# Hyena block with a gated FFN: down-weight loads at their own step of POOL's queue, first stage's tables redrawn

## The reference

```python
xn = layernorm(x)                                   # eps 1e-5
# attention branch: a second layernorm, with gamma and beta
proj = (layernorm(xn, gamma, beta) @ W_in + b_in)   # 256 -> 3 * 256: v, x1, x2
y = conv(v, k0) * x1                                # causal, 128 taps, per channel
y = conv(y, k1) * x2
attn = xn + (y @ W_out + b_out)
# FFN branch: integer weights times 1/127, hidden size 768
ffn = (silu(xn @ w_gate.T) * (xn @ w_up.T)) @ w_down.T
out = x + attn + ffn
```

## Time and profile before

| | us |
|---|---|
| median of 3 runs (325.54 to 327.3) | 325.62 |
| the profiled execution | 325.64 |
| its span | 323.7 |
| TensorE busy | 300.2 |
| VectorE busy | 264.6 |
| POOL busy | 210.0 |
| ScalarE busy | 184.4 |

### The profile page before, as it was taken

One profiled execution on the slowest core, in us unless ns is written; L12 is line 12 of the kernel. 1 busy time (PEld: TensorE's weight loads), 2 busy tenths in 40 slices (PEclk: granted clock), 3 DMA queues, 4 the chain that ended last, 5 costly groups with the idle time before them and its releaser, 6 DMA issues.

```text
span 323.7 us, 11895 instructions
## 1 busy us (share of the span) xinstructions
PE 300.2 (93%) x4945; PEld 235.9 (73%) x4945; DVE 264.6 (82%) x490; ACT 184.4 (57%) x398; POOL 210.0 (65%) x290
## 2 busy tenths in 40 slices
PE   0778999999999999999999999999999999999993
PEld 0366889977677777868777777877777867668982
DVE  2799999759886978886897989879787877879994
ACT  2769999644544445452554454354445344679990
POOL 4698997687877876968787776868778573100000
PEclk9999999999999999999999999999999999999998
DMA  7995005898796787869687687968678789002344
GB/s 229 350 349 113 2 0 149 371 374 339 283 377 230 316 299 270 357 225 382 205 337 276 281 315 253 375 220 367 232 306 309 276 357 330 26 1 68 132 165 163
DMA packets 22033, 81.01 MB, mean 250 GB/s; under 512 B 1494, under 2 KB 13402, under 8 KB 13786
## 3 DMA queue, kind: packets, MB, share of 16 engines
q1 hardware_dynamic: 19458, 77.47, 63.9%
q0 software_dynamic: 2368, 2.36, 3.7%
q10 hardware_dynamic: 152, 0.40, 0.4%
HBM read 75.50 MB, written 4.72 MB: 248 GB/s over the span
## 4 chain that ended last, share of the span: by engine, by line
PE 37%; POOL 18%; DVE 17%; issue 12%; ACT 11%; DMA 3%; POOLq 0%; SPq 0%; DVEq 0%
PE bank_c L324 12%; PE bank_p L324 7%; PE bank_u L324 5%; PE bank_g L324 5%; DVE sgh L1047 5%; PE bank_d L324 5%; POOL ybuf L1381 4%; ACT vx L838 4%; DVE hhl L1052 4%; ACT hhl L757 3%; POOL res L1333 3%; ACT vx L830 3%; DMA res<-in_L_attn_x 3%; POOL res L1334 2%; DVE ybuf L1068 2%
## 5 line engine op out<-in xcount | busy, mean ns | idle before, releaser
L324 PE MATMUL bank_d<-wd,hhl 128*128 128x256 f16 x384 | 84.2, 271 | 0.2 <-DVE res L1059 0.2
L324 PEld LDWEIGHTS bank_p<-wq,xT 128*128 128x128 f16 x1536 | 69.3, 98 | 14.1
L324 PE MATMUL bank_p<-wq,xT 128*128 128x64 f16 x1536 | 78.5, 193 | 0.0
L324 PE MATMUL bank_g<-xT,wgu 128*128 128x512 f16 x192 | 66.2, 377 | 0.5 <-ACT sgh L751 0.5
L324 PE MATMUL bank_u<-xT,wgu 128*128 128x512 f16 x192 | 66.2, 378 | 0.1
L324 PEld LDWEIGHTS bank_c<-ybuf,bands 128*128 128x128 f16 x1024 | 51.9, 96 | 17.3 <-issue 0.9
L324 PEld LDWEIGHTS bank_c<-vhl,bands 128*128 128x128 f16 x1024 | 48.9, 96 | 18.8 <-issue 3.4
L324 PE MATMUL bank_c<-ybuf,bands 128*128 128x64 f16 (+3 forms) x1024 | 60.5, 184 | 0.6 <-issue 0.6
L757 ACT CAST hhl<-sgh 128x512 f16<-128x512 f32 x48 | 29.7, 618 | 52.4 <-DVE sgh L1047 52.4
L324 PE MATMUL bank_c<-vhl,bands 128*128 128x64 f16 (+3 forms) x1024 | 57.4, 184 | 2.0 <-DVE ybuf L1068 1.0
L1052 DVE TENSOR_TENSOR hhl<-sgh,hhl 128x512 f16<-128x512 f32 x48 | 46.9, 977 | 13.9 <-ACT hhl L757 12.9
(11 more groups left out here) (185 smaller groups left out, 562.1 us busy)
## 6 DMA issues: line engine op xcount, KB each, us to landing
bands<-taps_seq SPq DMA_DIRECT2D x64, 1024.0 KB, 8.2
out<-res SPq DMA_DIRECT2D x8, 512.0 KB, 3.1
res<-in_L_attn_x SPq DMA_DIRECT2D x3, 1024.0 KB, 10.8
res<-in_L_attn_x SPq DMA_DIRECT2D x2, 512.0 KB, 6.1
bands<-in_L_attn_W_in SPq DMA_DIRECT2D x1, 768.0 KB, 6.0
wgu<-in_L_ffn_w_gate POOLq DMA_DIRECT2D x1, 768.0 KB, 8.8
wgu<-in_L_ffn_w_up POOLq DMA_DIRECT2D x1, 768.0 KB, 10.0
wd<-in_L_ffn_w_down POOLq DMA_DIRECT2D x2, 384.0 KB, 10.4
```

Source lines behind the costliest of these rows:

```text
L324: return nc.tensor.matmul(o, w, m, start=start, stop=stop, skip_group_check=True)
```

## The change

The two down loads are taken out of `load_integers` into a function `load_down` with a table entry of its own, INTS_DOWN = 2; INTS becomes 3. In the loop the call of `load_down` stands behind that of `load_integers`. The other tables of the stage get other entries: block 7, 17 and 22 are normalised by POOL, 23 by VectorE, 24 by ScalarE; x1 tile 5 goes to ScalarE and 6 to VectorE; the flip of the second batch moves from block 9 to 8 and second_scales(2) from step 11 to 9.

```diff
@@ -36,27 +36,28 @@
     CR = 32
     NR = D // CR
     CUTS = (0, 4, 8, 16, 24, NB)
-    V_LATE, V_EARLY = 8, 3
-    X_LATE, X_EARLY = 2, 5
+    V_LATE, V_EARLY = 9, 3
+    X_LATE, X_EARLY = 3, 5
     LAST = 44
-    FLIPS = (6, 9, 13, 19, 25)
-    NORM = "AAAAAAAAAPAPPAPPAAVPAAVPPAAPPAPP"
+    FLIPS = (6, 8, 13, 19, 25)
+    NORM = "AAAAAAAPAPAPPAPPAPVPAAPVAAAPPAPP"
     REVERSE = "AAAAAAAAAAVVAAVAVAAAAAAAAVAVAAAV"
-    X1 = "AAAAAVAAVVVVVVAV"
-
-    STATS = {1: 2, 3: 2, 4: 1, 5: 1, 6: 2, 9: 1, 10: 3}
-    WHI, WLO, PLO, SDG, KMAX = 2, 4, 2, 4, 4
-    BETA, BIAS = (2, 5), (5, 12)
-    SCALES_1, SCALES_2 = (5, 10, 18), (4, 8, 11, 15, 24)
-    INTS = 2
+    X1 = "AAAAAAVAVVVVVVAV"
+
+    STATS = {1: 1, 3: 2, 4: 2, 5: 1, 6: 1, 7: 1, 9: 1, 10: 2, 11: 1}
+    WHI, WLO, PLO, SDG, KMAX = 3, 4, 2, 4, 4
+    BETA, BIAS = (2, 4), (5, 12)
+    SCALES_1, SCALES_2 = (5, 10, 18), (4, 8, 9, 15, 24)
+    INTS = 3
+    INTS_DOWN = 2
     TAPS = (11, 16, 17, 23, 24)
     ADD_X2 = (29, 29, 39, 43)
-    ADD_BIAS, ROUND_V, SPLIT_V = (16, 20, 37, 43), (20, 24, 30, 37), (28, 31, 38)
-    MAXIMA = (7, 8, 8, 10, 12, 13, 16, 16, 16)
-    FLAG_PE, FLAG_V = (18, 19), (18, 21, 24, 29)
-    PAIR_PE = (22, 24, 29, 33, 39, 39, 39, 45, 48)
+    ADD_BIAS, ROUND_V, SPLIT_V = (16, 20, 36, 43), (20, 24, 30, 37), (28, 31, 38)
+    MAXIMA = (8, 8, 8, 10, 12, 14, 16, 16, 16)
+    FLAG_PE, FLAG_V = (18, 19), (18, 22, 24, 29)
+    PAIR_PE = (22, 24, 29, 33, 39, 39, 42, 45, 46)
     PAIR_A = (22, 24, 29, 33, 38, 39, 44, 48, 50)
-    PAIR_V = (23, 26, 32, 39, 39, 42, 45, 50, 51)
+    PAIR_V = (23, 26, 32, 37, 40, 42, 45, 50, 51)
     RESIDUALS = (0, 2, 2, 3, 2, 3, 3, 2, 2, 2, 2, 2, 2, 2, 2, 0)
     FORK = 24
     NBATCH = len(CUTS) - 1
@@ -1336,6 +1337,8 @@
             def load_integers():
                 pool.dma_start(gu_f[:, 0:HB, :], w_gate.rearrange("(u p) d -> p u d", p=P)).then_inc(int_loaded[0], 16)
                 pool.dma_start(gu_f[:, HB:2 * HB, :], w_up.rearrange("(u p) d -> p u d", p=P)).then_inc(int_loaded[1], 16)
+
+            def load_down():
                 for a in range(KD):
                     pool.dma_start(wd_f[:, :, a, :], w_down[a * P:(a + 1) * P, :].rearrange("p (j d) -> p j d", d=D)).then_inc(int_loaded[2], 16)
 
@@ -1344,6 +1347,8 @@
             for b in range(2, LAST):
                 if b == INTS:
                     load_integers()
+                if b == INTS_DOWN:
+                    load_down()
                 if b in SCALES_1:
                     first_scales(SCALES_1.index(b) + 2)
                 if b + 2 < NB and NORM[b + 2] == "P":
```

## The result

The changed kernel takes 327.86 us (median of 20 runs, 325.26 to 330.12), the kernel before 326.05 (20 runs, 325.08 to 330.5). The ratio is 1.0053, interval 1.0034 to 1.0072: slower by half a per cent, about 1.7 us. Forecast were 326.7 us and +1.1, with a range of 324.8 to 328.1. The measured 327.86 lies inside it, near the upper edge; the kernel before stood 0.4 us higher in these runs than the 325.62 from which the forecast started. The profiled execution took 326.52 us, its span is 324.7.

A forecast was written before the change was run, and what follows sets the result against it. Bound by TensorE from 33 to 62 us, before that by POOL's chain until 32.65. 325.64 us plus 1.30 + 0.35 - 0.19 - 0.37 = +1.1 gave 326.7 us, range 324.8 to 328.1.

The forecast's parts named there:

- The loads' order: POOL's four DMA issues, down loads first: 3.44 us in either order, gate landing near 25.6, nothing waits; 0 us.
- L945 where it stood, L1254 held up: VectorE's input-weight split again starts at 19.71; POOL's 8-number instruction beside it again lasts about 1.6 us; 0 us.
- rival A: POOL's chain 1.6 us shorter, for instance L1254 not held up (1.42); no wait at block 12; -0.5, 325.1 us; chance 0.18.
- Block 12 ready at 33.2, block 14 at 35.75: POOL normalises block 12 3.0 us later; TensorE waits 1.7 us there and starts block 14 1.30 us later.
- From block 14 to the end: TensorE's remaining work: +0.35 for two late v blocks, -0.19 and -0.37 for waits gone before blocks 18 and 24.
- rival B: ScalarE takes over the first stage's end, some 1.9 us late behind the first pair; stage 1.9 to 2.3 late, 327.7; chance 0.17.
- B's point of decision: TensorE needs block 23's split for block 26; ScalarE decides if it loses 1.5 us more than 1.9.
- The wait ahead of block 24 gone because of the flag: TensorE's 0.37 us wait goes because VectorE now splits block 21 ahead of the flag and scales.
- The sum: All terms together, TensorE's delay through the stage: +1.1 us, giving 326.7 us.
- the forecast's own band: Whole kernel slower by +0.6 to +1.6 us; chance 0.50.
- What moves the first convolution moves the end: TensorE's dense main loop passes on any shift at the first convolution; forecast wrong if the shift at 63 differs from the end's.

The follow-up runs named there:

- the second profile: The changed kernel, unaltered, profiled once more; first convolution at 63.68 us, against 64.06 in its first profile and 62.06 in the kernel before.
- flag run: Changed kernel with VectorE's flag and weight scales back at step 21 instead of 22; ratio 1.0035 (1.0006 to 1.0064).
- the kernel with the three entries back: Changed kernel with block 7 on ScalarE, second_scales(2) at step 11, second batch's flip at block 9 again; ratio 0.9999 (0.9974 to 1.0023).
- the three entries alone: Kernel before with only block 7 on POOL, second_scales(2) at step 9, second batch's flip at block 8; ratio 1.0023 (0.9995 to 1.0051).

## Why the prediction was right or wrong, point by point

- **The loads' order, 0 us.** Right: 3.49 and 3.48 us of issues, gate at 25.8 (forecast 25.6), ratio 1.0005 for it alone.
- **L945 where it stood, L1254 held up.** Right in the changed kernel (19.84; 1.55 us). The fear in rival A was justified: when VectorE starts 0.6 us later and POOL 0.4 earlier, L1254 isn't held up, 0.21 us. But what the prediction said of it, that an earlier L1254 would only hand the block to the power behind, is wrong. The power that began at 19.42 took its 1.64 us, and L946 beside it its 1.81; only the instruction behind the power was held, 0.63 us instead of 0.20. So 1.0 of the 1.42 us is gained.
- **Block 12 ready at 33.2, block 14 at 35.75.** Measured 33.24 (32.68 and 0.56) and 35.80 at full clock, with 1.50 us of standing (forecast 1.7). With the stands ahead of blocks 7 and 8 that the same three entries make, this step carries the result: taking the entries back brings 1.0053 to 0.9999, and block 14 to 34.51.
- **From block 14 to the end, forecast -0.2 us.** Mis-sized. At full clock the shift was +1.35 at block 14, +1.17 at block 24 (47.98 against 46.81), as summed, and then +1.62 at block 28 (53.36; before, 51.74) and at the first convolution. The 0.45 us more come from ScalarE being late. Its rounding of the first pair, block 23, and a reversal, from the second profile:

```profile
47.70 0.71 ACT L714 ACTIVATE wgu<-bank_d,cst 128x512 f16<-128x512 f32 x1
...
48.77 0.39 ACT L688 CAST xT<-bank_d 128x256 f16<-128x256 f32 x1
...
51.96 0.68 ACT L695 COPY xr<-xT 128x512 f16<-128x512 f16 x1
```

  The pair is 1.75 us later than before (45.95) and the rounding of block 23 at 48.77, where rival B said 48.9. B's point of decision (block 26) was not reached, but the reversal that ends at 52.64 releases the x1 product at 52.69, 0.28 us late (it is this wait, and not x1 tile 9, as the flag run's expectation had it). The other 0.16 lies ahead of block 25: the second pair's transposes wait until 49.2 for VectorE's split of the first pair, which could start only behind ScalarE's rounding of it. So a small part of rival B came true beside the forecast. In all, the step from block 14 to the first convolution measures +0.27 us (1.62 less 1.35) where -0.2 was forecast, and +0.55 in the kernel with the three entries back.
- **The wait ahead of block 24 gone because of the flag.** The wait went, the reason was wrong (flag back at step 21).
- **The clock.** Not foreseen. In the first profile it adds 0.4 us at the first convolution. The kernel before has no such fall in the stage (its mean of 0.995 comes from the last 4 us, with 0.59 granted). In the timed runs a lower clock is more frequent after the change: ten of 20 runs have a mean under 0.995, of the kernel before three to five in series of 29 to 35. (A mean doesn't say where in the run the clock fell.) But the loss is there without it: the five runs with a mean of 0.999 took 327.41, 327.68, 328.03, 329.05 and 329.32 us, none of them near the 326.05 of the kernel before.
- **The sum.** +1.6 us at full clock and +2.0 with the dip, against +1.1; the times say 1.7. That is just above the forecast's own band of +0.6 to +1.6 and inside the range given with it. The mechanism was right up to block 14, and what was missed is the half microsecond behind it.
- **What moves the first convolution moves the end.** The prediction named it as a sign of being wrong if the two shifts differ, and in both profiles they do: +2.0 at the first convolution and +1.0 at the end in the first, +1.6 and +2.8 in the second. No edit reaches beyond the first group of the main loop. The difference is made there, by stops that nothing explains (below) and by POOL's split of v, for which TensorE stands 0.28 us near 85 in the profile before and 0.55 in both after, but 0.54 with the load order alone too. The median of 20 runs, not one profile, carries the result.

What stays open: why the three entries alone, on the kernel before, give only 1.0023. Their profile caught the other order of L1254 and L945; whether they do so in most runs was not tried, nor is it known why the lower clock goes with longer times there and not in the changed kernel.

## What to carry to other kernels

When a queue is rewritten, add up, for each consumer, the time at which its input is released, in the queue's new order; a step moved forward (second_scales(2)) delays all that it passes (block 12), and TensorE, which runs its queue in order, stands there with other work behind it. When time is taken out of one queue, check next the engine that has no idle time beside it: time taken out of POOL's chain ended in a wait for VectorE's statistics. And one profile isn't a measurement of 0.5%: repeat it before a difference inside it is explained.

## What the runs showed of the hardware that was not expected

**The port between POOL and VectorE.** The Trainium skill (page SBUF — State Buffer, section SBUF: two separate sides) says that a VectorE instruction with two SBUF inputs and a GpSimd (POOL) one that reads SBUF share a port pair, and that whichever starts first has it for the whole instruction while the other is blocked. One way round the rows agree: L1255 on POOL, begun 0.3 us behind L946, lasts 1.55 instead of 0.21 us and ends with it, 21.7 (changed kernel, first profile). The other way round they don't: with the down loads at step 12, a power over 8 columns (19.42 to 21.06) had begun first, reads SBUF, and VectorE's L946 with two inputs in SBUF ran from 19.89 in its usual 1.81 us. The kernel with the three entries shows the same (power from 19.83, L945 from 20.30). The next POOL instruction, at 21.14, was held again until L946's end (0.63 instead of 0.20 us). The measurement decides: the long arithmetic of a short POOL operand did not keep VectorE out.

**A stop of TensorE that waits for nothing shown.** In the first group's second convolution TensorE stands in the midst of a channel, in the kernel before and in some profiles of the others, with no wait that the profile names; kernel before, then the changed kernel's second profile:

```profile
69.22 0.24 PE L324 MATMUL bank_c<-ybuf,bands 128*128 128x62 f16 x3 [0.56 <-issue]
```

```profile
71.75 0.23 PE L325 MATMUL bank_c<-ybuf,bands 128*128 128x62 f16 x3 [1.43 <-issue]
```

The first profile of the changed kernel has none. That is 0.56 us of the way from its +2.0 at the first convolution to +1.0 at the end; TensorE gets back a further 0.8 us in small steps between the groups that start at 173 and 244 us, and loses 0.27 at POOL's split. Other profiles have such stops later, 1.19 us before 250.47 with block 7 back on ScalarE and 0.57 before 235.26 with the load order alone. No semaphore, load or engine is named for them; their cause is open. They are of the size of the effect under study.

**The clock level isn't fixed by the program.** One program, two profiles: 0.50 and 1.00 granted from 24 to 30 us. TensorE's stand just ahead was the same (1.78 and 1.77 us); the one before that was 1.04 us in the first and 0.47 in the second.
